# Graph network kernel: the last edge's row of each node is picked out on chip by one-hot products, and node work runs inside the edge passes

## The reference

```python
def _egnn_conv(x, src, dst, edge_attr, W_msg, W_edge, W_root, b):
    msg = x[src] @ W_msg + edge_attr @ W_edge          # 32 edge features
    agg = segment_max(msg, dst)
    return agg + x @ W_root + b
x = _layernorm(x + leaky(conv(leaky(conv(x)))))        # two convolutions: passes 0 and 1

h = relu(edge_attr_17 @ W1.T + b1)                     # pass 2
w = h @ W2.T + b2
agg = segment_sum(w * x[src], dst)
x = _layernorm(x + relu(x @ Ws.T + bs + agg @ Wn.T + bn))

# two hops with deg^-1/2 on both sides, then one hop with its own degrees and a weight:
# three products with the adjacency (the "dense hops"), each segment_sum(norm * h[src], dst)
```

## Time and profile before

| what | value |
| --- | --- |
| median of three runs | 5130.83 us |
| span of the profiled execution | 5118.6 us |
| the runs' times | 5130.24, 5130.83, 5136.9 us |
| PE, PE weight loads | 4044.6 us (79%), 2656.8 us |
| DVE, ACT, POOL busy | 2232.8 (44%), 1002.8 (20%), 2581.0 us (50%) |
| moved by DMA | 695.04 MB |
| chain that ended last | PE 59%, unknown queue 14%, DVE 12%, issue 10% |

### The profile page before, as it was taken

The page is one execution under the profiler, slowest core; times in us unless marked ns, Lnnn a source line. Parts: engine busy times, 40 slices in busy tenths (PEclk is TensorE's granted clock), DMA queues, the critical chain, the costliest instruction groups (busy, mean ns, idle before and its releaser), DMA issues.

```text
span 5118.6 us, 56111 instructions
## 1 busy us (share of the span) xinstructions
PE 4044.6 (79%) x19316; PEld 2656.8 (52%) x19316; DVE 2232.8 (44%) x5877; ACT 1002.8 (20%) x2108; POOL 2581.0 (50%) x2689
## 2 busy tenths in 40 slices
PE   5777767677368776777764998998898969999999
PEld 4333333333333333333333655555555649999999
DVE  3454555555124444444443555555555552222211
ACT  1100000000122222222223333333333330001101
POOL 4666666665556666666655665566566530000000
PEclk9999999999965667666655566556666559999999
DMA  5333333333234444444432443434343327777776
GB/s 136 100 99 89 102 95 100 89 101 88 48 93 136 124 135 127 137 121 138 131 100 66 117 122 114 123 115 123 110 127 108 117 84 268 269 266 268 263 260 219
DMA packets 251432, 695.04 MB, mean 136 GB/s; under 512 B 80458, under 2 KB 163082, under 8 KB 219914
## 3 DMA queue, kind: packets, MB, share of 16 engines
q1 hardware_dynamic: 56126, 348.35, 21.2%
q0 software_dynamic: 85568, 131.83, 12.0%
q10 hardware_dynamic: 109516, 212.06, 11.4%
HBM read 477.94 MB, written 214.09 MB: 135 GB/s over the span
## 4 chain that ended last, share of the span: by engine, by line
PE 59%; another core or an unknown queue 14%; DVE 12%; issue 10%; ACT 2%; DMA 1%; POOL 1%; DVEq 0%; ACTq 0%; POOLq 0%; SPq 0%
PE banks L1118 17%; PE banks L981 9%; PE banks L1022 7%; PE banks L976 6%; PE banks L956 6%; PE banks L947 5%; PE banks L995 5%; DVE scan L1831 5%; DVE hot_lo L1483 3%; DVE hot_hi L1485 1%; PE banks L735 1%; DVE hot_key L1848 1%; DVE hot_src L1850 1%; ACT adj L1350 1%
## 5 line engine op out<-in xcount | busy, mean ns | idle before, releaser
L709 POOL DMA_INDIRECT gath<-table,ids x2496 | 2406.3, 964 | 1425.4 <-issue 698.5
L1831 DVE TENSOR_TENSOR_SCAN scan<-keep_of,scan,banks 96x512 f32<-96x512 bf16 x621 | 791.3, 1274 | 1737.9 <-remote 972.9
L1118 PE MATMUL banks<-r_parts,adj_in 128*128 128x288 bf16 x7203 | 890.2, 286 | 5.1 <-DVE r_parts L1531 2.6
L1118 PEld LDWEIGHTS banks<-r_parts,adj_in 128*128 128x128 bf16 x7203 | 883.2, 142 | 7.4 <-DVE r_parts L1531 3.4
L995 PEld LDWEIGHTS banks<-ident,scan 96*128 96x128 f32 x2496 | 400.9, 224 | 911.7 <-issue 505.7
L995 PE MATMUL banks<-ident,scan 96*128 96x96 f32 x2496 | 528.4, 359 | 325.7 <-DVE scan L1831 254.5
L981 PE MATMUL banks<-ea_of,w_edge_of 32*96 32x512 f32 x832 | 765.1, 1016 | 0.3 <-issue 0.3
L1022 PE MATMUL banks<-hot_key,hot_src 128*128 128x392 bf16 x1600 | 543.3, 475 | 272.8 <-issue 139.3
L1332 ACT ACTIVATE back<-banks 128x384 f32<-128x384 f32 x624 | 305.2, 489 | 2062.0 <-remote 873.4
L1848 DVE TENSOR_SCALAR hot_key<-iota_key,key_t 128x392 bf16<-128x392 int16 x1600 | 505.4, 316 | 21.0 <-ACT key_t L1371 21.0
L956 PEld LDWEIGHTS banks<-w_edge_out,hid 97*128 97x128 f32 x1664 | 320.2, 287 | 307.2 <-issue 305.4
(11 more groups left out here) (158 smaller groups left out, 2100.9 us busy)
## 6 DMA issues: line engine op xcount, KB each, us to landing
adj_in<-adjacency SPq DMA_DIRECT2D x147, 1568.0 KB
scanned_rows<-back ACTq DMA_DIRECT2D x153, 768.0 KB
adjacency<-adj ACTq DMA_DIRECT2D x100, 784.0 KB
gath<-table,ids POOLq DMA_INDIRECT x2496
ea_of<-in_ea_t SPq DMA_DIRECT2D x78, 512.0 KB
keep_of<-keep_max_d SPq DMA_DIRECT2D x52, 768.0 KB
keep_of<-keep_sum_d SPq DMA_DIRECT2D x26, 768.0 KB
table<-x_sb SPq DMA_DIRECT2D x10, 240.0 KB, 4.4
```

What stands on the lines that cost most here:

```text
L709: pool.indirect_dma_start(gath[:, b, t, :], None, tables[p][:, :], bass.IndirectOffsetOnAxis(ap=ids[:, 1, n:n + 1], axis=0),).then_inc(s_g ...
L1118: m = pe.matmul(sum_ps[:, u, j, :], adj_in[:, a, :, h], r_parts[:, n % 2, h, :, :].rearrange("p k f -> p (k f)"), start=h == 0, stop=h == ...
L1831: ve.tensor_tensor_scan(scan[0:D, b, at:at + Q], keep_of[:, i % 2, CHUNK * b + at:CHUNK * b + at + Q], turn_ps[k % 2], start, keep_op, tak ...
```

## The change

The scanned rows no longer go to DRAM. The nodes are taken in 49 blocks of 128. On average 17 edge tiles (`PER`) belong to a block, and the program takes it that a border between two blocks lies within 6 tiles (`MARGIN`) of its mean place; it tests this at the start and takes a general path where it does not hold. A tile thus adds to one block, or near a border to two: 29 products for 17 tiles. `rel_end` holds for each edge its node's place in a span of two blocks where the edge is the last of its node, and a value outside the span where it isn't. `hots_in_span` compares it with 0..255 and gives a one-hot, `to_blocks` multiplies it (as weights, 128x128) with the rows (128x96) and sums in PSUM until the block's last tile.

In pass 2 the sum over edges is made by the same products with the one-hots of all edges: its scan, turn and turn back are gone, and `msg_now` goes into the product.

Node work runs for one block at a time as soon as the block's last tile is in, some steps after it (`blocks_at`), between the quarters' work. The two windows of a quarter now share one PSUM bank and stand apart in PE's order. The reading of the keys for the adjacency moves from the node phase after pass 0 to the first pair of pass 1.

```diff
+PER = 17
+MARGIN = 6
+def blocks_of(tile):
+    base, place = base_of(tile), tile % PER
+    both = (base,) if MARGIN <= place < PER - MARGIN else (base, base + 1)
+    return [h for h in both if 0 <= h < BLOCKS]
...
+        back1_ps = banks[:, 0, 0:QT * D]
+        seg_ps = [banks[:, b, 0:D] for b in (2, 3)]
-        window_ps = [banks[:, b, 0:KEYS] for b in (2, 3)]
+        window_ps = banks[:, 6, 0:KEYS]
+        wide_w_ps = [banks[:, b, 0:QT * D] for b in (4, 5)]
...
+        def blocks_at(p, s, later):
+            ready = s - later - (LAG + 1 if IS_MAX[p] else 0)
+            return ending(ready) if 0 <= ready < QUARTERS else []
...
+                    def store_block(h):
+                        sp.wait_ge(s_y[1] if p == 0 else s_node[2], h + 1)
+                        sp.dma_start(tables_v[p + 1][:, h, :], (y if p == 0 else node)[:, h % 2, 0, :])\
+                          .then_inc(s_table[p + 1][h % 2], 16)
...
+                def to_blocks(p, q, rows_in):
+                    for t in range(QT):
+                        tile = QT * q + t
+                        for h in blocks_of(tile):
+                            if tile == first_tile(h) and (p > 0 or h >= 2):
+                                pe.wait_ge(s_seg_out, BLOCKS * p + h - 1)
+                            c = P * (h - base_of(tile))
+                            m = pe.matmul(seg_ps[(BLOCKS * p + h) % 2], hot_dst[:, q % 2, t, c:c + P],
+                                          rows_in[:, q % 2, t * D:(t + 1) * D],
+                                          start=tile == first_tile(h), stop=tile == last_tile(h), skip_group_check=True)
+                    m.then_inc(s_sel, 1)
+                def select_ends(p, q):
+                    pe.wait_ge(s_evac, QUARTERS * p + q + 1)
+                    pe.wait_ge(s_hot_end, QUARTERS * p + q + 1)
+                    to_blocks(p, q, back_of)
...
+                    for s in range(QUARTERS + TAIL):
+                        for i, k in windows_at(p, s, 1):
+                            count_window(p, i, k, 0)
+                        if LAG <= s < QUARTERS + LAG:
+                            turn_back(p, s - LAG)
+                        if LAG < s <= QUARTERS + LAG:
+                            select_ends(p, s - LAG - 1)
+                        if p == 0 and LAG <= s < QUARTERS + LAG:
+                            count(s - LAG)
+                        for h in blocks_at(p, s, 1 if p == 0 else 4):
+                            turn_node(p, h)
+                        for i, k in windows_at(p, s, 1):
+                            count_window(p, i, k, 1)
+                        if s < QUARTERS:
+                            turn(p, s)
+                        for h in blocks_at(p, s, 2 if p == 0 else 5):
+                            multiply_node(p, h)
...
+                def evacuate(p, q):
+                    act.wait_ge(s_back, QUARTERS * p + q + 1)
+                    if p > 0 or q >= 2:
+                        act.wait_ge(s_sel, QUARTERS * p + q - 1)
+                    act.activation(back_of[:, q % 2, :], back1_ps, ACT.Copy).then_inc(s_evac, 1)
-                        if g == 3 or last_chunk:
-                            n = 1 if last_chunk else 4
-                            act.wait_ge(s_evac, base + 8 * i + k - LAG + 1)
-                            act.dma_start(rows_v[:, bass.ds(8 * turn_i + g8 - n + 1, n), :],
...
+                def hots_in_span(q, of):
+                    return ve.tensor_tensor(hot_dst[:, q % 2, :, :],
+                                            of[:, QT * q:QT * (q + 1)].unsqueeze(2).to_broadcast([P, QT, SPAN]),
+                                            span_ps.unsqueeze(1).to_broadcast([P, QT, SPAN]), ALU.is_equal)
```

More of the change, by code:

```diff
@@ new lines, in turn_back @@
+                def turn_back(p, q):
+                    i, k, base = quarter_of(p, q)
+                    pe.wait_ge(s_scan, base + q + 1)
+                    if p > 0 or q > 0:
+                        pe.wait_ge(s_evac, base + q)
+                    if p == 1 and q == 0:
+                        pe.wait_ge(s_start, 1)
+                    at = Q * (k % 4)
+                    for t in range(QT):
+                        m = pe.transpose(back1_ps[:, t * D:(t + 1) * D], scan[0:D, k // 4, at + t * P:at + (t + 1) * P],
+                                         ident[0:D, 0:D])
+                    m.then_inc(s_back, 1)
@@ new lines, in count_window @@
+                def count_window(p, i, k, j):
+                    n = WINDOWS * BUILT * (p - 1) + WINDOWS * i + 2 * k + j
+                    pe.wait_ge(s_window_hot, n + 1)
+                    if n > 0:
+                        pe.wait_ge(s_window_out, n)
+                    for a in range(KEY_TILES):
+                        m = pe.matmul(window_ps, hot_src[:, 2 * (k % 2) + j, a, :], hot_key[:, 2 * (k % 2) + j, a, :],
+                                      start=a == 0, stop=a == KEY_TILES - 1)
+                    m.then_inc(s_window_mm, 1)
@@ new lines, in _ @@
+                for p in range(2):
+                    if p == 0:
+                        pe.wait_ge(s_weights, 16 * (len(loads) - 3))
+                    else:
+                        pe.wait_ge(s_deg, 1)
+                        pe.matmul(before_ps[:, 0:NT], upper[:, :], deg[:, :], start=True, stop=True)
+                        pe.matmul(before_ps[:, NT:2 * NT], ones[:, :], deg[:, :], start=True, stop=True).then_inc(s_prefix, 1)
+                    for s in range(QUARTERS + TAIL):
+                        for i, k in windows_at(p, s, 1):
[14 more added lines that the diff above has]
+                            multiply_node(p, h)
+                        if s == KEYS_AT:
+                            (turn_lines if p == 0 else turn_keys)()
@@ new lines, in hidden, with edge_rows @@
+                def hidden(q):
+                    i, k, _ = quarter_of(2, q)
+                    columns, weights = edge_columns(i, k)
+                    if k == 0:
+                        pe.wait_ge(s_ea[i % 2], 16 * pair_loaded(2, i))
+                    if q >= 1:
+                        pe.wait_ge(s_hid, q)
+                    pe.matmul(hid1_ps, weights(2), columns, start=True, stop=True).then_inc(s_hid_ps, 1)
+                def edge_rows(q):
+                    pe.wait_ge(s_hid, q + 1)
+                    if q >= 2:
+                        pe.wait_ge(s_msg, q - 1)
+                    for t in range(QT):
+                        m = pe.matmul(wide_w_ps[q % 2][:, t * D:(t + 1) * D], hid[:, q % 2, t * P:(t + 1) * P],
+                                      W["edge_out"][:, :], start=True, stop=True)
+                    m.then_inc(s_w, 1)
@@ new lines, in sum_quarter @@
+                def sum_quarter(q):
+                    pe.wait_ge(s_msg, q + 1)
+                    to_blocks(2, q, msg_now)
+                hidden(0)
+                hidden(1)
+                edge_rows(0)
+                hidden(2)
+                edge_rows(1)
+                for s in range(QUARTERS + TAIL):
+                    for i, k in windows_at(2, s, 1):
+                        count_window(2, i, k, 0)
+                    if s + 3 < QUARTERS:
+                        hidden(s + 3)
+                    for h in blocks_at(2, s, 2):
+                        turn_node(2, h)
+                    if s + 2 < QUARTERS:
+                        edge_rows(s + 2)
+                    for i, k in windows_at(2, s, 1):
+                        count_window(2, i, k, 1)
+                    if s < QUARTERS:
+                        sum_quarter(s)
+                    for h in blocks_at(2, s, 3):
+                        multiply_node(2, h)
@@ L1391, in _ @@
+                for p in range(2):
+                    if p == 1:
                         act.wait_ge(s_deg, 2)
@@ L1447, in _ @@
             ve.memset(eps[:, :], EPS)
+            ve.memset(strays[:, :], 0.0)
             ve.memset(ends[:, NT:], 0)
@@ L1531, in into_parts, with nodes @@
                 return ve.tensor_tensor(third, left, second, ALU.subtract)
-            def nodes(p, dense=False):
+            def nodes(p):
                 n = p + 1
```

766 lines of the change are left out of this document (439 added, 327 removed).

## The result

The changed kernel takes 6204.12 us in the median of four runs (6181.71 to 6223.81) against 5130.53 for the kernel before: a ratio of 1.21, with a 95% interval of 1.2061 to 1.2139. Forecast were 5770 us and at most 6080. The direction was right, the cause was not.

What follows compares the result with a forecast made beforehand. PE, mostly at 1.2 GHz, was taken to bound all three passes. Start, passes, borders and hops summed to 6045 us without clock rises, 5492 with the earlier shares; about the middle, 5770, was forecast, range 4850 to 6080.

Steps and rivals of the forecast that it cites:

- All are over POOL's 5.00, so PE sets all three passes: PE's quarters at 1.2 GHz, 7.38, 8.20 and 8.32 us by pass, exceed POOL's 5.00, so PE bounds each.
- the others are shorter. It is hidden: DVE's quarter, at most 5.2 us in the first pass and shorter in the others, lies under PE's work.
- signs of being wrong: Second-pass clock over 0.75, products at 0.25 us, first-pass PE waits for select one-hots or ACT copy, border over 60 us.
- the first and the third pass: Passes over the edges, forecast as PE's time at 1.2 GHz: 208 quarters of 7.38 us, 1535, and of 8.32, 1720.
- The cost of a select product: Each f32 to_blocks product on PE takes 0.455 us at 1.2 GHz, 0.243 at 2.4; 3.08 us a quarter at 1.2.
- The clock: PE's time share at 2.4 GHz: none in the first pass, between none and 0.24 and 0.22 in the later ones.
- the 55 us at 0.50: From 3330 to 3385 us PE was fully busy at granted clock 0.50, so full load alone brings no rise.
- The third: Rival: all three passes run at 2.4 GHz and POOL sets them; 4464 us (4200 to 4720), chance 0.10.
- The first: Rival: clock rises and stays in second and third pass, POOL sets both; 4876 us (4706 to 5050), chance 0.20.
- The second: Rival: a select product costs what a transpose does, 0.25 us; 5178 us without clock rises, chance 0.05.
- the fourth: Rival: fall-back path taken because a block border strays over 6 tiles; far over any range, chance called nil.
- the price of what goes: 153 stores and 26 loads of 768 KB dropped; they lie beside PE's work, so nothing was counted for them.

Runs made afterwards that it cites:

- e1: Changed kernel, with DVE making the second pass's window one-hots ahead of the scan, not behind it: 4509.67 us, ratio 1.0146 to the kernel before.
- f2: Changed kernel, DVE as it is, PE and ACT taking the second pass's window products one quarter later: 5474.05 us, ratio 1.0801 to the kernel before.
- c1: Changed kernel unedited, run again on a chip where the kernel before takes about 4440 us: 5539.99 us, ratio 1.2455.
- e2: e1 with add_ends (adding up a finished block) also ahead of the scan on DVE: 4238.42 us, ratio 0.9526 to the kernel before.
- e4: e2 with four of five select products left out, their rows missing from the result: 4340.6 us, ratio 0.9759 to the kernel before.
- e3: e2 with select products in bf16, the rows' lower 16 bits left out of the result: 4369.94 us, ratio 0.9837 to the kernel before.
- f1: e2 with PE's wait for the last weights moved from the first pass's head to the first block's products: 5232.41 us, ratio 1.0338 to the kernel before.
- c2: Kernel before the change, unedited, run again for its trace on the faster kind of chip: 4433.74 us.
- h1: f1 with two PSUM banks for window products, the second and third pass's compare reading 0..255 from SBUF: 5048.52 us, ratio 0.9956 to the kernel before.

## Why the prediction was wrong

**The step that failed** is "All are over POOL's 5.00, so PE sets all three passes": it takes a pass's quarter as the largest of the engines' own times. In the second pass the quarter is the sum of PE's and DVE's, 10.0 us, because of the order in which each runs its step. Of DVE's work in the second pass the prediction says "the others are shorter. It is hidden": it compares lengths, and does not ask what PE's first instruction of a step waits for and what stands ahead of that on DVE. In the kernel before, the window one-hots stood ahead of the scan; in the changed one they stand behind it, and the sentence ahead of the prediction that "the scan and the window one-hots stand as before" is wrong. This puts the second pass 600 us over its term, more than the whole miss of 434 us; e1 and f2 show it. None of the signs of being wrong that the prediction names would have shown it. The same failed in the first pass in small: each block's add_ends stands behind the scan (183 us of waits in c1, 265 us of time with the clock's part).

**Near by luck** were the first and the third pass (1409 for 1535, 1535 for 1584). They were forecast as PE's own time, and PE is idle for 19 and 21% of them. In c1 the same two passes take 1289 and 1037 us, the third at POOL's floor. So "PE sets all three passes" did not hold as written in any: what brought the third pass near its term is what the 5100 chips lose, which the forecast doesn't have.

**The cost of a select product** was right, and beside the point. At the two levels of the clock in the profile after:

```profile
703.74 1.95 PE L1066 MATMUL banks<-back 128*128 128x96 f32 x16
705.53 0.36 PE L1082 MATMUL banks<-hot_hi,hot_lo 128*128 128x50 bf16 x8
...
722.47 3.62 PE L1066 MATMUL banks<-back 128*128 128x96 f32 x16
725.88 0.54 PE L1082 MATMUL banks<-hot_hi,hot_lo 128*128 128x50 bf16 x8
```

8 products take 1.79 and 3.41 us, 0.224 and 0.426 each, for 0.243 and 0.455. But in e2 the passes stand at POOL's floor with all of them in.

**The clock** was the second wrong term. I took the before-kernel's share at 2.4 GHz as the most to be had, and for the first pass none. It rose in all three, in the first without any window product (edge matmuls of 1.09 us near 702 beside 2.02 near 720). The argument from the 55 us at 0.50 was too weak: those were other products, on fewer partitions; whether that is the reason was not tried. That the rises follow the window products in one block is refuted by the first pass. On one chip the third pass reads 0.90 with the added f32 products (e2), 0.58 with most of them out (e4) and 0.57 with bf16 in their place (e3). For the Trainium skill's sentence (TensorE: Matmul & The Clock Gate, "What's actually happening"), by which activity releases the throttle, the verdict turns: in e2 PE is 90 to 96% busy in the passes and the clock reads 0.84 to 0.90, near what I had dismissed. In e4's third pass, though, PE is 96% busy and reads 0.58, so activity alone doesn't tell the reading here.

**The rivals.** The third (clock up in all three passes, POOL sets them, faster than before) is what the change does once the waits are out and on a 4440 chip: ratio 0.9526 in e2, at 0.84, 0.89 and 0.90. On a 5100 chip the same order of work takes 5232 us (f1), more than before, so the rival's 4464 us is not met there. With the waits in, it could not come about. The first has it for the second and third pass only, and e2 shows it in the first too. The first one's range should read 4710 to 5042 us by its own terms, not 4706 to 5050; nothing hangs on that. The second was wrong (a select costs 0.43 at 1.2 GHz, not 0.25), and so was the fourth, for all 4224 select products are in the trace.

**Right were** the borders (35 and 36 us for 35), the hops, the price of what goes (nothing to be seen inside the passes: c2 and e2 have the same, though both at POOL's floor, where a price could hide), and the compare on DVE (1.19 us for 1.3). The start was 22 us short, through the wait for w_l. The key reads keep PE waiting 61 us in the profile after and 26 in c1; the sum had nothing for them, and the text some 20 us if the clock were high.

**Open**: what makes completions late on some chips. Both kernels as they were compared lose nearly the same by it, so it does not make the ratio of 1.21. A version without the waits loses more: 4238 us in e2 and 5232 in f1, which is 5% faster than before on one kind of chip and 3% slower on the other. That would fit more hand-overs between engines that have to come in time, as does the second PSUM bank with the 4% that h1 wins back, but which of the others count was not tried.

## What to carry to other kernels

When work is moved between loops that are written out for each engine, follow one step around all engines: for the first instruction of a step, ask what it waits for and what stands ahead of that on the other engine. A quarter costs the largest of the engines' times only if no such round closes; else it costs their sum. Here the kernel with such rounds took 1.25 of the time before (c1), and without them 0.95 (e2). And price a change on more than one chip when many small hand-overs lie in it.

## What the runs showed of the hardware that was not expected

Taking PE work away can lengthen a pass: with four of five f32 select products left out, or with bf16 ones in their place, the third pass took 1140 and 1166 us instead of 1036, at a granted clock of 0.58 and 0.57 instead of 0.90. The same kernel takes 4434 us on one chip and 5131 on another, 16% more, and its times agree within about 1% on each; each chip was used in one stretch of time. On the slow kind DVE started 56 us after the end of the matmul that it waited for, and POOL came free at the same moment. An indirect gather on POOL, 0.94 us as a rule, took 1.32 us on average and up to 2.56 where it overlapped a compare of DVE that read both operands from SBUF (h1). And POOL was idle for 3.0 us on average at a drain behind four indirect gathers.
